# Three of six second-layer products of the last mixture of experts written as fp32r triples, with the low halves subtracted on GpSimd

## The reference, cut to what matters

```
rh = relu(features @ router_w1 + router_b1)
expert_logits = softmax(rh @ router_w2 + router_b2)
top_w, top_i = top_k(expert_logits, 2)
routing_weights = softmax(top_w)
h1 = relu(einsum('bsd,edh->bseh', features, expert_w1) + expert_b1)   # 6 experts, 128 -> 128
h2 = relu(einsum('bseh,ehf->bsef', h1, expert_w2) + expert_b2)        # the second layer
expert_out = einsum('bsef,efo->bseo', h2, expert_w3) + expert_b3
combined = sum(take_along_axis(expert_out, top_i) * routing_weights)
```

## Time and profile before

| what | us |
|---|---|
| median of 3 runs | 855.92 |
| lowest and highest | 854.97, 860.66 |
| the profiled execution, its own time | 854.43 |
| its span, first to last instruction | 852.5 |
| TensorE busy in the span | 811.2 (95%) |
| VectorE, ScalarE, GpSimd busy | 697.4, 521.3, 426.0 |

### The profile page before, as it was taken

The page is one execution under the profiler, slowest core; times in us unless marked ns, Lnnn a source line. Parts: engine busy times, 40 slices in busy tenths (PEclk is TensorE's granted clock), DMA queues, the critical chain, the costliest instruction groups (busy, mean ns, idle before and its releaser), DMA issues.

```text
span 852.5 us, 21598 instructions
## 1 busy us (share of the span) xinstructions
PE 811.2 (95%) x6244; PEld 624.2 (73%) x6245; DVE 697.4 (82%) x2699; ACT 521.3 (61%) x1120; POOL 426.0 (50%) x413
## 2 busy tenths in 40 slices
PE   7998999999788899999999999899999999999997
PEld 7675777777547899999999999566665655555563
DVE  4899988989867798877777888888888888888863
ACT  3666787786645466556565654556566656655664
POOL 4248888888877300940100042566665566666300
PEclk9899999999999999999999999999999999999999
DMA  9602411131115766676666762344443344443323
GB/s 269 178 12 78 114 52 48 54 112 42 45 42 171 201 189 174 172 194 167 174 170 163 176 181 75 111 123 124 122 124 120 118 138 147 152 131 121 108 88 99
DMA packets 107591, 108.25 MB, mean 127 GB/s; under 512 B 27822, under 2 KB 89600, under 8 KB 105344
## 3 DMA queue, kind: packets, MB, share of 16 engines
q1 hardware_dynamic: 96976, 88.52, 36.4%
q0 software_dynamic: 8880, 18.19, 7.0%
q10 hardware_dynamic: 1664, 0.66, 0.3%
HBM read 82.07 MB, written 25.26 MB: 126 GB/s over the span
## 4 chain that ended last, share of the span: by engine, by line
PE 61%; issue 4%; POOL 3%; DVE 1%; DMA 1%; ACT 0%; SPq 0%; POOLq 0%; DVEq 0%
PE banks L2073 16%; PE banks L2113 10%; PE banks L2237 10%; PE banks L2229 9%; PE banks L2205 7%; PE banks L2088 2%; PE banks L2134 2%; PE banks L2145 1%; PE banks L2162 1%; PE banks L2251 1%; PE banks L2174 1%; POOL slots_in L1292 1%; POOL expert_rows L1352 1%; PE banks L2154 1%; DMA slots_out<-ys 0%
## 5 line engine op out<-in xcount | busy, mean ns | idle before, releaser
L1352 POOL DMA_INDIRECT expert_rows<-slots_out,slot_c x128 | 140.8, 1100 | 74.6 <-DVE ys L1610 42.1
L326 POOL DMA_INDIRECT slots_in<-flat,slot_now x115 | 120.7, 1050 | 35.7 <-issue 31.2
L2073 PE MATMUL banks<-xT_hi,w_hi 128*128 128x256 f32 (+1 forms) x426 | 127.0, 298 | 0.4 <-DVE w_lo L1629 0.4
L2073 PE MATMUL banks<-xT_hi,w_lo 128*128 128x256 f32 (+1 forms) x426 | 120.7, 283 | 0.0
L2073 PE MATMUL banks<-xT_lo,w_hi 128*128 128x256 f32 (+1 forms) x426 | 120.4, 283 | 0.0
L2113 PE MATMUL banks<-w_sb,prod 128*128 (+1 forms) x852 | 107.1, 275 | 2.4 <-DVE ys L1610 2.4
L2113 PEld LDWEIGHTS banks<-w_sb,prod 128*128 128x128 f32 (+1 forms) x852 | 101.3, 191 | 2.8 <-issue 2.6
L2073 PEld LDWEIGHTS banks<-xT_hi,w_hi 128*128 128x128 f32 (+1 forms) x426 | 76.2, 179 | 0.6 <-issue 0.6
L2073 PEld LDWEIGHTS banks<-xT_lo,w_hi 128*128 128x128 f32 (+1 forms) x426 | 76.6, 180 | 0.0
L2073 PEld LDWEIGHTS banks<-xT_hi,w_lo 128*128 128x128 f32 (+1 forms) x426 | 76.2, 179 | 0.0
L1426 ACT ACTIVATE w_hi<-w_raw 128x684 fp32r<-128x684 f32 x71 | 54.9, 773 | 26.3 <-PE banks L2073 26.3
(11 more groups left out here) (306 smaller groups left out, 2116.7 us busy)
## 6 DMA issues: line engine op xcount, KB each, us to landing
w_raw<-in_w SPq DMA_DIRECT2D x71, 342.0 KB, 3.4
f_all<-gates_dram SPq DMA_DIRECT2D x16, 1024.0 KB, 6.7
xs<-slots_in SPq DMA_DIRECT2D x71, 128.0 KB, 2.6
slots_out<-ys SPq DMA_DIRECT2D x71, 128.0 KB
f_all<-gates_dram SPq DMA_DIRECT2D x16, 512.0 KB, 4.5
base_all<-in_x SPq DMA_DIRECT2D x16, 256.0 KB, 4.2
out<-ob SPq DMA_DIRECT2D x16, 256.0 KB
slots_in<-zrow SPq DMA_DIRECT2D x20, 128.0 KB, 3.5
```

What stands on the lines that cost most here:

```text
L326: G.indirect_dma_start(out=slots_in, out_offset=bass.IndirectOffsetOnAxis(ap=slot_now0[g % 2][:, n:n + 1], axis=0), in_=flat[g % 2][:, n / ...
L1352: G.indirect_dma_start(out=rows[p][:, n, :], out_offset=None, in_=slots_out[0:filled(g) * R, :], in_offset=bass.IndirectOffsetOnAxis(ap=sl ...
L2073: last = T.matmul(banks[bank][0:m, half * R:(half + 1) * R], ww[:, par, n * HIDP + c * P:n * HIDP + c * P + m], xx[:, par, :], start=q == ...
```

## The change

The second layer of experts 1, 2 and 4 becomes three fp32r products each: high weights by high `h1`, low weights by high `h1`, high weights by low `h1`. The weights' halves are made once by GpSimd, three casts and three subtractions of 128x128 more, at about 354 us. ScalarE runs its relu twice for these experts, once into an fp32r buffer and once into fp32. GpSimd subtracts the one from the other, once for each expert and group (`low(2)`, `low(1)`, `low(4)`), after gt(7) and ahead of rstd1. The third product waits for this subtraction. `h1` of experts 1 and 4 get buffers of their own, and ScalarE's order changes: ra1 moves ahead of the gates' copies, ra4 moves to the step before, ep ahead of rb3.

```
+                        for i, n in enumerate(SPLIT):
+                            G.tensor_copy(ew2_hi[:, i * C:(i + 1) * C], ew2[:, n * C:(n + 1) * C]).then_inc(prepared, 1)
...
+                    def low(n, g):
+
+                        if g is not None:
+                            pool.wait_ge(per["ra"].sem, per["ra"].at(f"ra{n}", g))
+                            G.tensor_tensor(h1_lo[n], h1[n], h1_hi[n].bitcast(f32), ALU.subtract).then_inc(per["l"].sem, 1)
+
                     def body(g, p):
                         gt(7, g[1], p[1])
+                        low(2, g[3])
+                        low(1, g[3])
+                        low(4, g[3])
...
+                            if n in SPLIT:
+                                S.activation(h1_hi[n], banks[B_A[n]][:, :], ACT.Relu, bias=eb1[:, n:n + 1])
+                            S.activation(h1[n][:, :], banks[B_A[n]][:, :], ACT.Relu, bias=eb1[:, n:n + 1]).then_inc(per["ra"].sem, 1)
...
                         ra(0, g[1])
                         rb(5, g[2])
+                        ra(1, g[1])
                         gTc(g[1], p[1])
-                        ra(1, g[1])
                         rb(0, g[1])
                         ra(3, g[1])
                         oTc(g[2])
                         rb(1, g[1])
                         hi(later(g[0], 1), p[0])
-                        ra(4, g[1])
                         ra(5, g[1])
                         rb(2, g[1])
                         rhr(g[0])
                         rb(4, g[1])
+                        ra(4, g[0])
                         etop_(g[0])
                         ra(2, g[0])
+                        ep_(g[0])
                         rb(3, g[1])
-                        ep_(g[0])
...
-                            T.matmul(banks[B_B[n]][:, :], ew2[:, n * C:(n + 1) * C], h1[n % 3][:, :], start=True, stop=True).then_inc(per["b"].sem, 1)
+                            w = ew2[:, n * C:(n + 1) * C]
+                            if n in SPLIT:
+                                w_high = ew2_hi[:, SPLIT.index(n) * C:(SPLIT.index(n) + 1) * C]
+                                T.matmul(banks[B_B[n]][:, :], w_high, h1_hi[n], start=True, stop=False)
+                                T.matmul(banks[B_B[n]][:, :], ew2_lo[:, SPLIT.index(n) * C:(SPLIT.index(n) + 1) * C], h1_hi[n], start=False, stop=False)
+                                low = per["l"]
+                                pe.wait_ge(low.sem, low.at(f"l{n}", g))
+                                T.matmul(banks[B_B[n]][:, :], w_high, h1_lo[n], start=False, stop=True).then_inc(per["b"].sem, 1)
+                            else:
+                                T.matmul(banks[B_B[n]][:, :], w, h1[n][:, :], start=True, stop=True).then_inc(per["b"].sem, 1)
```

More of the change, by code:

```diff
@@ L1068, in build @@
             DEG_BLOCK, degrees = 8, sem("degrees")
-            PREPARED = 8 + TG - 1
+            SPLIT = (1, 2, 4)
+            PREPARED = 8 + TG - 1 + 2 * len(SPLIT)
             st_a, mv_a, var_a, rs_a = sb("st_c", [P, TG, 6]), sb("mv_c", [P, TG, 2]), sb("var_c", [P, TG]), sb("rs_c", [P, TG])
@@ L1077, in build @@
             h1 = [w[:, 1, 0:2, :].rearrange("p c r -> p (c r)") for w in (act1, prod)] + [sb("h1_2", [P, GT])[:, :]]
+            h1 = [h1[0], h1[1], h1[2], h1[0], xs[:, 2:4, :, :].rearrange("p u t c -> p (u t c)"), h1[2]]
             h2 = [f[:, :, :].rearrange("p t c -> p (t c)") for f in flat] + [act1[:, 0, 0:2, :].rearrange("p c r -> p (c r)")]
@@ L1081, in build @@
             oT = sb("oT", [P, GT])
+            ew2_hi, ew2_lo = sb("ew2_hi", [P, len(SPLIT) * C], f32r), sb("ew2_lo", [P, len(SPLIT) * C], f32r)
+            h1_hi = dict(zip(SPLIT, (w_hi[:, 0, 0:GT], w_hi[:, 1, 0:GT], w_lo[:, 0, 0:GT])))
+            h1_lo = dict(zip(SPLIT, (w_lo[:, 1, 0:GT], xT_hi[:, :, :].rearrange("p t r -> p (t r)"), xT_lo[:, :, :].rearrange("p t r -> p (t r)"))))
             gateT = [sb(f"gateT{i}", [P, P]) for i in range(2)]
@@ L1107, in build @@
                 ("a4", "a2", "a1", "a0", "a3", "a5"),
-                ("ra2", "ra0", "ra1", "ra3", "ra4", "ra5"),
+                ("ra4", "ra2", "ra0", "ra1", "ra3", "ra5"),
                 ("b0", "b1", "b2", "b3", "b4", "b5"),
                 ("rb0", "rb1", "rb2", "rb4", "rb3", "rb5"),
+                ("l2", "l1", "l4"),
                 ("m0", "m1", "m2", "m3", "m4", "m5"),
@@ L1453, in ra @@
                             act.wait_ge(per["a"].sem, per["a"].at(f"a{n}", g))
-                            reused(act, "b", n, g)
-                            S.activation(h1[n % 3][:, :], banks[B_A[n]][:, :], ACT.Relu, bias=eb1[:, n:n + 1]).then_inc(per["ra"].sem, 1)
+                            if n in (1, 4):
+                                if has(g - 1):
+                                    act.wait_ge(per["b"].sem, per["b"].at(f"b{n}", g - 1))
+                            else:
+                                reused(act, "b", n, g)
+                            if n in SPLIT:
+                                S.activation(h1_hi[n], banks[B_A[n]][:, :], ACT.Relu, bias=eb1[:, n:n + 1])
+                            S.activation(h1[n][:, :], banks[B_A[n]][:, :], ACT.Relu, bias=eb1[:, n:n + 1]).then_inc(per["ra"].sem, 1)
                     def rb(n, g):
```

10 lines of the change are left out of this document (7 added, 3 removed).

## The result

The changed kernel takes 880.34 us (median of 6 runs, 877.95 to 882.2), the kernel before 856.31 beside it. That is a ratio of 1.0287 (1.0267 to 1.0308), 24 us slower, where the prediction had 9 and a range that ended at 871. The span of the profiled execution grew from 852.5 to 877.7 us.

What follows compares the result with a forecast made beforehand. TensorE looked like the price, busy all step, but three places in its order wait on other engines. 14 steps at +0.65 make +9.1, less 0.3: +8.8 on 855.9, forecast 864.8 us, range 853 to 871.

Steps and rivals of the forecast that it cites:

- What they do to VectorE: GpSimd's subtractions block VectorE's two-SBUF-input m4 and m5, taking turns with them; f3T 0.81 us late, step +0.65.
- The walk from it: Last stage, from aT: low1 ends 6.06 us, m4 6.61, low4 7.76, m5 8.31, so f3T is 0.81 late.
- rival 2: GpSimd keeps its turn between low1 and low4: m4 ends 7.90, m5 9.2, +1.5 us a step, 877; chance 0.07.
- the forecast's 20.0: Sign expected in the changed trace: last-stage steps of 20.0 us, with f3T 11.8 us behind aT.
- 0.65 a step: Each step's growth in us: rh 0.81 late through VectorE's delay, less 0.16 that b4 gives back.
- The sum: 14 steps at +0.65 make +9.1 us, last full step and drain save 0.3: +8.8, forecast 864.8.
- The product: On TensorE an fp32 product takes 0.86 us, an fp32r triple 0.70: 0.16 goes for each expert.
- Its covers: TensorE's b1 and b2 savings become waits ahead of oT and rh; only b4 counts, 0.16 us a step.
- -2.6: Rival that GpSimd and VectorE hardly meet: b4's 0.16 us in 15 steps and 0.2 in the drain, 853.3; chance 0.17.
- The exclusion: VectorE with two SBUF inputs and GpSimd reading SBUF exclude each other for a whole instruction; x3, with PSUM input, not blocked.
- The third longer than 1.29: Sign expected on GpSimd: the third subtraction, low4, blocked by m4, takes more than 1.29 us.
- rs_d idle near zero to 1.5: Sign expected on GpSimd: idle time at rs_d, behind the subtractions, near zero to 1.5 us.

Runs made afterwards that it cites:

- experiment 9: Changed kernel with the third subtraction, low4, cut into two instructions of 128 and 384 columns: 879.6 us (one run).
- Experiment 1: Changed kernel without the three subtractions, the third product reading the high half of h1 again: 853.87 us, ratio 0.9966 to the kernel before.
- experiment 3: Changed kernel with a short GpSimd memset of 128x64 between the second and third subtractions, low1 and low4: 880.9 us, ratio 1.0303.
- experiment 5: Changed kernel with a longer GpSimd memset of 128x512 between low1 and low4: 875.33 us, ratio 1.0236.
- experiment 10: Changed kernel with one wait, for ra1, ahead of all three subtractions and none between, so they also start later: 866.72 us (one run).
- experiment 13: Changed kernel with a wait for ra1 ahead of all three subtractions, the waits between them kept: 870.97 us (one run).
- experiment 14: Changed kernel with one wait ahead of the subtractions, none between, started later by a tiny addition and a 128x255 memset: 875.74 us (one run).
- experiment 15: Changed kernel with the subtractions started later by a tiny addition and a 128x255 memset, waits between them kept: 878.88 us (one run).
- experiment 12: Changed kernel cut to expert 4 alone as a triple, with no subtraction (its low half left out): 853.94 us, ratio 0.9969.
- experiment 2: Changed kernel with a one-column addition and a 128x511 memset in place of each subtraction, low halves left out: 853.53 us, ratio 0.9979.
- experiment 4: Changed kernel with the second layer in single fp32 products again, subtractions and the rest kept: 881.62 us, ratio 1.0316.
- experiment 18: Changed kernel with only the wait ahead of the third subtraction, low4, left out: 879.31 us (one run).
- experiment 17: Changed kernel with a 128x512 memset between low2 and low1, nothing between low1 and low4: 888.11 us (one run).
- experiment 16: Changed kernel with low2 on 384 of its 512 columns, waits and order unchanged: 871.86 us (one run).
- experiment 8: Changed kernel with the subtractions spread between the gathers, low4 after gt(5), low2 after gt(6), low1 after gt(7): 922.12 us, ratio 1.0754.
- experiment 6: Changed kernel cut to expert 4 alone as a triple with one subtraction, order of the rest kept: 858.49 us, ratio 1.0033.
- experiment 11: Expert 4 alone with its one subtraction, the next to last group's held back until the last group's xn is made: 858.77 us, ratio 1.0034.

## Why the prediction was wrong, and where it was right

**The step that failed** is the one in "What they do to VectorE": "between two back-to-back GpSimd instructions the waiting VectorE one got in". It rested on one pair, rw_lo of the earlier trace rows and the subtraction ahead of it:

```profile
354.60 1.85 POOL L1327 TENSOR_TENSOR ew_lo<-f_all,ew_hi 128x768 fp32r<-128x768 f32 x1
```

The second of the pair had 128 columns, and the third subtraction here has 512; experiment 9 shows that this matters. The walk from it had m4 end at 6.61 us behind aT and m5 at 8.31. In the changed kernel low1 and low4 ran without a gap, m4 ended at 7.74, and m5, which met nobody, at about 9.1. So f3T moved by 1.6 us and not by 0.81. This is the mechanism of rival 2, given 7 in 100: it had m4 at 7.90, m5 at 9.2, 1.5 a step and 877 us. Experiment 1 shows that the subtractions are the whole loss. Experiments 3 and 5 show that it hangs on VectorE not getting in between the second and the third: with a break of 0.51 us there the ten steps in which m4 got in were the forecast's 20.0 on average. Experiments 10 and 13 to 15 show the turns that the forecast had assumed, when m4 meets the first subtraction. Their price is higher than its 0.65 a step: 0.9 over the kernel before in 10 and 13, and 1.3 in 14 and 15. What makes the difference there is not shown.

**The sum, term by term.** The steady steps that kept their clock are at 20.8 to 21.0 (the eleventh at 21.8), 1.4 to 1.6 above the mean of before: rival 2's number. Two steps behind waits of 1.87 and 1.92 us add 1.9 each by the clock, a term that no case of the prediction had. The filling of the stage adds 2.3, where the sum had 0.65 for it. Part of this is the clock too: TensorE waited 2.24 us for f3 there, and behind that its granted clock was 0.50 from 552 to 554 us. In experiment 3, which kept 1.00, the filling took 17.78, 1.0 less. The first full step adds nothing: there m4 asked just 0.13 us before low1's end and got in. So rival 2's total of 877 comes near 880 partly by luck: it counted 1.5 us for the first full step, and left out the clock. (The forecast's own total is 0.1 off: 855.9 and 8.8 make 864.7.)

**What held.** The product: 0.70 a triple. Its covers: experts 1 and 2 gave nothing (experiment 12 against 1). The rest of the change without the subtractions: -2.4 where -2.6 was worked out. The subtractions' length: 1.25 to 1.28 where 1.29 was taken. They fitted into GpSimd's idle time, and this said nothing of their price. The exclusion held as well: m4 ended 0.55 behind the subtraction that it waited for, and x3, with one input in PSUM, was unharmed. ScalarE's relus, GpSimd's waits and TensorE's waits inside the triples: no cost in the full steps (experiments 1, 2, 4 and 18). "The third longer than 1.29" and "rs_d idle near zero to 1.5" were wrong in the change, and they were the signs by which it could be told: 1.25 and 2.69 us.

**Which engine waits.** The Trainium skill ("SBUF — State Buffer", Who interferes with whom) says that the engine that issues first blocks the other. By the rows of GpSimd and VectorE above this does not foretell what happened: m4's row began 0.50 us before low4's, and low4 ran first.

**What stays open.** What decides whether a waiting VectorE instruction gets in between two GpSimd ones that read. It is not the semaphore waits (13, 15, 18), not the distance alone (14 and 15 against the change: 0.53 to 0.65 ahead, in and out), and not the place in an unbroken run (17). The length of the next piece has a part in it (9), but does not decide alone. Two differences are left. In 10 and 13 to 15 GpSimd stood idle for about 0.55 us or more behind its last gather, while in the change the subtractions follow the gather directly. The other is that low1 took its turn unhindered behind low2 in the change, while in experiments 10 and 13 to 15 it had waited for m4 before m5 got in behind it. In experiment 16 a difference of 0.01 us in the asking time went with opposite outcomes. Whether the gather ahead of the run makes the claim of the queued subtractions earlier, as experiment 8 suggests, was not tried by itself. Open is also where experiments 6 and 11 lose 4.6 and 4.8 us against experiment 12: their steps agree to 0.03 us on average. Of the 5.3 us between the profiled spans of 11 and 12, 3.5 lie ahead of the stage, where the code is the same, 0.9 in the filling, where 11 shows a granted clock of 0.90 and 12 one of 1.00, 0.1 in the 13 steps behind that, and 0.8 in the drain.

No version beat the kernel before with all of the work done. The best with all three terms of a triple was expert 4 alone, 858.49, a ratio of 1.0033 (1.0005 to 1.006).

## What to carry to other kernels

Idle time on GpSimd is free only for what VectorE doesn't exclude: before moving a wide two-input instruction there, list VectorE's instructions with two SBUF inputs in that window (experiments 8 and 13 show two with one input that were shut out as well), and price each meeting at the end of the whole queued run on GpSimd, not at the end of the instruction that it meets. One such meeting seen elsewhere in a trace is not the rule for the order in the next. If it must go there, keep it single and clear of those instructions (experiment 6 against the change: 22 us), or see whether a later start lets VectorE in behind the first of them (some 13 us in the one run of experiment 10). Neither made the change pay here.

## What the runs showed of the hardware

- Between two 1.25 us GpSimd subtractions a waiting VectorE instruction was kept out in all 12 steady steps of the change, 2.3 to 2.6 us in place of 0.68; with a next piece of 128 columns it got in in 6 of 12. A break of 0.14 us by a memset did not help, and one of 0.51 helped in 10 of 12 steps.
- A queued subtraction shut VectorE out up to 0.69 us before its own row began, while a gather ahead of it ran (experiment 8). There a TENSOR_SCALAR with one input of 128x4 was kept out as well, 1.49 us in place of 0.15. In experiments 13 and 15 a copy of 128x8, 0.14 us in the steady steps of the change, took 0.94 beside low4.
- A memset of 128x511 took 0.52 us on GpSimd, and m4, begun 0.1 us before its end, kept its 0.68. In experiment 5 m4 and a memset of 128x512 overlapped by 0.46 us without harm to either.
- In the change, behind TensorE's two waits of 1.87 and 1.92 us, its granted clock fell to near the lower level for some 3.7 us, and about 1.9 us more were lost each time; behind its waits of 1.61 to 1.75 us it stayed up. The length of the wait does not tell it by itself: in experiment 3 the clock stayed up behind waits of 1.95 and 2.02 us, and in experiment 17 it fell behind five of 2.11 to 2.34 us and stayed up behind five of 2.08 to 2.22.
